# Two-layer attention and dense kernel: inverse roots of twelve norm chunks on DVE in place of ACT, and the first dense transposes ahead of an output projection

## The reference

```python
def _layernorm(x, axis=-1, eps=1e-05):
    m = jnp.mean(x, axis=axis, keepdims=True)
    v = jnp.var(x, axis=axis, keepdims=True)
    return (x - m) / jnp.sqrt(v + eps)
...
x = x + attn_a(_layernorm(x))   # 32 heads of 8, biases, softmax over all 1024 keys
x = x + ffn(_layernorm(x))      # silu(x @ w_gate) * (x @ w_up), 2 of each 4 kept by size, @ w_down
x = x + attn_b(_layernorm(x))   # 32 query heads, 8 key/value heads, a band of 128 keys masked
x = x + ffn(_layernorm(x))      # the same dense layer again
```

## Time and profile before

| | before |
|---|---|
| runs, median | 1659.77 us |
| the profiled execution, time | 1661.77 us |
| its span | 1659.80 us |
| PE busy | 1609.1 us, 97% |
| DVE busy | 1491.0 us, 90% |
| ACT busy | 1281.8 us, 77% |
| POOL busy | 266.8 us, 16% |
| mean granted PE clock | 0.991 |

### The profile page before, as it was taken

How to read it: one execution, slowest core, us unless ns; L and a number is a source line. 1 busy time by engine, 2 the same in 40 slices (tenths; PEclk the granted TensorE clock), 3 DMA queues, 4 the chain that set the end, 5 groups by cost and what they waited for, 6 DMA issues and landing times.

```text
span 1659.8 us, 39596 instructions
## 1 busy us (share of the span) xinstructions
PE 1609.1 (97%) x14128; PEld 636.9 (38%) x14128; DVE 1491.0 (90%) x2168; ACT 1281.8 (77%) x2424; POOL 266.8 (16%) x623
## 2 busy tenths in 40 slices
PE   6899999999999999999988999999999999999999
PEld 3322222222222223787653222222222222237877
DVE  6999999999999997787678999999999999937765
ACT  3399999999999998433224999999999999983321
POOL 1410000000000000000012222333332233320000
PEclk9989999999999999999998999999999999999999
DMA  6943344334354321200404232222222322112000
GB/s 160 296 98 70 63 76 84 63 64 84 69 139 87 73 60 44 64 1 0 117 15 132 59 66 57 51 51 65 57 55 62 62 57 51 55 49 58 14 13 26
DMA packets 72126, 114.70 MB, mean 69 GB/s; under 512 B 12464, under 2 KB 27824, under 8 KB 71984
## 3 DMA queue, kind: packets, MB, share of 16 engines
q1 hardware_dynamic: 71984, 112.63, 29.2%
HBM read 71.96 MB, written 40.63 MB: 68 GB/s over the span
## 4 chain that ended last, share of the span: by engine, by line
PE 54%; DVE 35%; issue 7%; ACT 1%; DMA 1%; SPq 0%; DVEq 0%; POOLq 0%; ACTq 0%
DVE mneg L1306 28%; PE psum L785 18%; PE psum L767 11%; PE psum L737 7%; PE psum L887 5%; PE psum L843 5%; PE psum L848 2%; PE psum L700 2%; PE psum L823 2%; PE psum L720 1%; PE psum L682 1%; DVE area L1356 1%; DVE area L1390 1%; DVE stats L1199 1%; DVE area L1340 1%
## 5 line engine op out<-in xcount | busy, mean ns | idle before, releaser
L1055 ACT ACTIVATE area<-psum 128x512 f32<-128x512 f32 x2048 | 1097.2, 600 | 42.1 <-PE psum L767 13.7
L785 PE MATMUL psum<-area 128*32 128x256 f32 x8192 | 655.2, 392 | 0.4 <-POOL area L1568 0.4
L767 PE MATMUL psum<-area 51*128 51x512 bf16 x2048 | 639.2, 385 | 2.5 <-DVE vsb_b L1256 1.4
L1312 DVE CUSTOM_DVE_ANT_0 xn<-psum,band 128x1024 f32<-128x1024 f32 x512 | 588.4, 1220 | 10.3 <-PE psum L737 9.3
L1306 DVE TENSOR_REDUCE mneg<-psum 128x1 f32<-128x1024 f32 x512 | 581.0, 1211 | 7.0 <-PE psum L737 6.9
L785 PEld LDWEIGHTS psum<-area 128*32 128x32 f32 x8192 | 162.1, 108 | 400.7 <-issue 259.1
L737 PE MATMUL psum<-area 48*128 48x512 bf16 x1024 | 301.6, 385 | 8.2 <-DVE mneg L1306 5.1
L767 PEld LDWEIGHTS psum<-area 51*128 51x128 bf16 x2048 | 141.0, 94 | 427.0 <-ACT area L1055 353.3
L737 PE MATMUL psum<-k_max_b,area 48*128 48x512 bf16 x1024 | 292.8, 385 | 5.4 <-DVE mneg L1312 4.7
L1549 POOL TENSOR_TENSOR mparts<-mneg,nought 128x16 bf16<-128x16 f32 x64 | 14.1, 221 | 742.3 <-DVE mneg L1306 501.1
L1100 ACT ACTIVATE area<-psum 128x512 f32<-128x512 f32 x64 | 38.2, 599 | 115.9 <-PE psum L848 115.8
(11 more groups left out here) (89 smaller groups left out, 1092.1 us busy)
## 6 DMA issues: line engine op xcount, KB each, us to landing
ctx_rows<-area SPq DMA_DIRECT2D x64, 256.0 KB, 2.1
area<-q_stacks SPq DMA_DIRECT2D x32, 384.0 KB, 6.8
area<-k_stacks SPq DMA_DIRECT2D x64, 192.0 KB, 5.6
area<-q_stacks_b SPq DMA_DIRECT2D x32, 384.0 KB, 5.3
area<-q_stacks SPq DMA_DIRECT2D x32, 192.0 KB, 4.6
area<-q_stacks_b SPq DMA_DIRECT2D x32, 192.0 KB, 3.4
area<-ctx_rows SPq DMA_DIRECT2D x16, 256.0 KB, 4.1
area<-inv_rows SPq DMA_DIRECT2D x16, 256.0 KB, 4.5
```

Source lines behind the costliest of these rows:

```text
L767: pe.matmul(psum[:, BANK_OF["exp", g, u, head], :], k_st[lo:lo + ROWS + PARTS, buf, 0 if a else head // 2, kt * P:(kt + 1) * P], q_st[lo:l ...
L785: mm = pe.matmul(psum[head * VW:(head + 1) * VW, BANK_OF["ctx", g, qh], cols], vaug[:, buf, kt, head, :], probs[:, u % PRING, head, cols], ...
L1055: act.activation(probs[:, u % PRING, head, :], psum[:, BANK_OF["exp", like, u, head], :], ACT.Exp, scale=SCALE).then_inc(bank_freed, 1)
L1312: dve.tensor_tensor_reduce(band_out[:, c % 2, :], slot, band[:, at:at + SEQ], 1.0, -3.0e38, ALU.add, ALU.max, mneg[:, qh, col:col + 1]).th ...
```

## The change

For k = 1, 2 and 3 ACT's square root and DVE's reciprocal are gone. In their place DVE's `invert_deviation` adds eps to the variance, makes a first guess of the inverse root from the bits of the number taken as an integer, and improves it by three Newton steps of three instructions each: eleven instructions on 128 x 4 elements, each of which waits for the one before (`root_step`). ACT's calls of `norm` for k = 1 to 3 go, k = 0 stays as it was. On PE `norm_transpose(2a + 1, 0)` now stands ahead of `project_out(a, 1)`, and on DVE `residue(2a + 1, 0)` ahead of `add_attention(a, 1)`. No DMA is added, removed or moved.

```diff
--- before.py
+++ after.py
@@ -20,6 +20,7 @@
 F32 = mybir.dt.float32
 BF16 = mybir.dt.bfloat16
 F32R = mybir.dt.float32r
+I32 = mybir.dt.int32
 ALU = mybir.AluOpType
 ACT = mybir.ActivationFunctionType
 AX = mybir.AxisListType
@@ -37,6 +38,8 @@
 SCALE = 1.0 / float(HD) ** 0.5
 EPS = 1e-5
 INNER = 1024
+FIRST_ROOT = 1597463007.0
+ROUNDS = 3
 BANK = 512
 HALF = SEQ // BANK
 
@@ -186,6 +189,8 @@
         mv = sb("mv", [P, BT, 2])
         std = sb("std", [P, BT])
         rstd = sb("rstd", [P, BT])
+        root_square = sb("root_square", [P, BT])
+        root_gain = sb("root_gain", [P, BT])
         eps = sb("eps", [P, 1])
         ident = sb("ident", [P, P])
         ident_bf = sb("ident_bf", [P, P], BF16)
@@ -318,7 +323,7 @@
         const_ready = sem("const_ready")
         const_step, ones_set, vaug_set = sem("const_step"), sem("ones_set"), sem("vaug_set")
         ln_stats, ln_mv, ln_sd, ln_rstd, ln_xn = (sem(s) for s in ("ln_stats", "ln_mv", "ln_sd", "ln_rstd", "ln_xn"))
-        ln_tr, ln_evac = sem("ln_tr"), sem("ln_evac")
+        ln_tr, ln_evac, root_step = sem("ln_tr"), sem("ln_evac"), sem("root_step")
         whole_hi, whole_split, xd_split = sem("whole_hi"), sem("whole_split"), sem("xd_split")
         proj_ready, hi_done, rest_done, mid_done, lo_done = (
             sem(s) for s in ("proj_ready", "hi_done", "rest_done", "mid_done", "lo_done"))
@@ -942,8 +947,8 @@
                 project_v(0, 0, v)
             for a in range(2):
                 attend(a)
+                norm_transpose(2 * a + 1, 0)
                 project_out(a, 1)
-                norm_transpose(2 * a + 1, 0)
                 if a == 0:
                     pe.wait_ge(wf_loaded, 48)
                 gate_up(a, 0, 0)
@@ -993,7 +998,7 @@
             def norm(k, c):
                 n, lo = 4 * k + c, c % 2 * CT
                 act.wait_ge(ln_mv, n + 1)
-                if n == 0:
+                if c == 0:
                     act.wait_ge(const_ready, 1)
                 act.activation(std[:, lo:lo + CT], mv[:, lo:lo + CT, 1], ACT.Sqrt, bias=eps[:]).then_inc(ln_sd, 1)
 
@@ -1121,7 +1126,6 @@
                     group(a, 2 * i + 1, 1)
                     group(a, 2 * i + 2, 2)
                 group(a, GROUPS - 1, GROUPS - 1, ahead=False)
-                norm(2 * a + 1, 0)
                 copy_ctx(a, GROUPS - 1, 1, GROUPS - 1)
 
             norm(0, 0)
@@ -1147,22 +1151,16 @@
             for a in range(2):
                 attend(a)
                 copy_transposed(2 * a + 1, 0)
-                norm(2 * a + 1, 1)
                 silu_and_size(a, 0, 0)
                 copy_transposed(2 * a + 1, 1)
                 silu_and_size(a, 0, 1)
                 silu_and_size(a, 1, 0)
-                norm(2 * a + 1, 2)
-                norm(2 * a + 1, 3)
                 silu_and_size(a, 1, 1)
                 copy_transposed(2 * a + 1, 2)
                 copy_transposed(2 * a + 1, 3)
-                if a == 0:
-                    norm(2, 0)
                 silu_and_size(a, 2, 0)
                 if a == 0:
                     copy_transposed(2, 0)
-                    norm(2, 1)
                     for i in range(3):
                         split_step(1, 0, i)
                 silu_and_size(a, 2, 1, turned=None if a else (2, 1))
@@ -1172,11 +1170,9 @@
                 silu_and_size(a, 3, 0)
                 silu_and_size(a, 3, 1)
                 if a == 0:
-                    norm(2, 2)
                     copy_transposed(2, 2)
                     for i in range(3):
                         split_step(1, 1, i)
-                    norm(2, 3)
                     copy_transposed(2, 3)
                     copy_turned(1, 0, 0, 0)
                     for i in range(3, PCH[1] + 1):
@@ -1203,12 +1199,36 @@
                     ins = dve.bn_aggr(mv[:, lo + t, :], stats[:, lo + t, :])
                 ins.then_inc(ln_mv, 1)
 
+            def invert_deviation(k, c):
+
+                n, cols = 4 * k + c, slice(c % 2 * CT, c % 2 * CT + CT)
+                s0 = (1 + 3 * ROUNDS) * (n - CH)
+                v, y, t, g = std[:, cols], rstd[:, cols], root_square[:, cols], root_gain[:, cols]
+                dve.wait_ge(ln_mv, n + 1)
+                dve.tensor_scalar(v, mv[:, cols, 1], EPS, None, ALU.add).then_inc(root_step, 1)
+                dve.wait_ge(root_step, s0 + 1)
+                dve.tensor_scalar(y.bitcast(I32), v.bitcast(I32), -0.5, FIRST_ROOT, ALU.mult, ALU.add
+                                  ).then_inc(root_step, 1)
+                for i in range(ROUNDS):
+                    dve.wait_ge(root_step, s0 + 3 * i + 2)
+                    dve.tensor_tensor(t, y, y, ALU.mult).then_inc(root_step, 1)
+                    dve.wait_ge(root_step, s0 + 3 * i + 3)
+                    dve.scalar_tensor_tensor(out=g, in0=t, scalar=-0.5, in1=v, op0=ALU.mult,
+                                             op1=ALU.mult).then_inc(root_step, 1)
+                    dve.wait_ge(root_step, s0 + 3 * i + 4)
+                    ins = dve.scalar_tensor_tensor(out=y, in0=g, scalar=1.5, in1=y, op0=ALU.add, op1=ALU.mult)
+                    ins.then_inc(ln_rstd if i == ROUNDS - 1 else root_step, 1)
+
             def scale(k, c):
                 n, lo = 4 * k + c, c % 2 * CT
-                dve.wait_ge(ln_sd, n + 1)
+                if k == 0:
+                    dve.wait_ge(ln_sd, n + 1)
                 if k == 2 and c == 2:
                     dve.wait_ge(stacks_stored[9], SD)
-                dve.reciprocal(rstd[:, lo:lo + CT], std[:, lo:lo + CT]).then_inc(ln_rstd, 1)
+                if k == 0:
+                    dve.reciprocal(rstd[:, lo:lo + CT], std[:, lo:lo + CT]).then_inc(ln_rstd, 1)
+                else:
+                    invert_deviation(k, c)
                 dve.wait_ge(ln_rstd, n + 1)
                 for t in range(CT):
                     if n >= 2 and t % 2 == 0:
@@ -1448,8 +1468,8 @@
                     dve.wait_ge(x_biased, 1)
                 add_attention(a, 0)
                 norm(2 * a + 1, 0)
+                residue(2 * a + 1, 0)
                 add_attention(a, 1)
-                residue(2 * a + 1, 0)
                 norm(2 * a + 1, 1)
                 invert_sums(a, 1)
                 hidden(a, 0, 0, follower=(0, 1))
```

## The result

| | runs shown | median | lowest to highest |
|---|---|---|---|
| kernel before, beside it | 6 | 1660.3 us | 1659.49 to 1665.77 |
| changed kernel | 6 | 1680.51 us | 1677.18 to 1683.82 |

The ratio is 1.0115, 95% interval [1.0103, 1.0127]: slower by some 20 us, where +10.6 was forecast. The direction was right, the size missed, and the range too. Three of the changed kernel's six times lie near 1677.4 and three near 1683.7; the profiled execution, 1683.82 with a span of 1681.8, is one of the longer ones.

What follows compares the result with a forecast made beforehand. It took PE (97% busy) and DVE's waits as the bound, not ACT's load; +8.30 us in the first dense layer and +2.33 in the second made +10.6 on 1659.77, so 1670.4 us, range 1665.8 to 1674.8.

Steps and rivals of the forecast that it cites:

- What bounds the kernel: Whole kernel: PE busy 97%, with 54% of the chain, DVE 35%, ACT 1%; ACT's load no bound, added DVE time can lose.
- (2,0): First dense layer, norm 2's first chunk: removed loads give DVE 0.59 us, scaling costs 1.89 more, so PE waits +1.30 us.
- (2,1): First dense layer, norm 2's second chunk: ACT's projection copy no longer stands behind the root, PE's idle goes, -0.68 us.
- The price of a Newton chain: On DVE, each norm chunk: eleven dependent instructions of 0.19 us, 2.12 us from last aggregation to scaling.
- 99 d - 8.2: Total change in us over nine chunks on the chain, d being the length of one Newton instruction; +13.1 at 0.215.
- (1,0), (3,0) and the order: Both dense layers' openings: chain fits DVE's idle time, gate matmuls start earlier, first gated product later: +0.82 and +0.87 us.
- (1,2) and (1,3): First dense layer, norm 1's last two chunks: both chains delay PE's row r2 at 736.48, +3.08 us.
- (2,2) and (2,3): First dense layer, norm 2's last two chunks: PE already idles behind DVE, each pays 1.89 in full, +3.78 us.
- (3,2) and (3,3): Second dense layer, norm 3's last two chunks: 3.08 us on DVE, less 1.62 of PE slack, +1.46 us.
- Rival 2: Newton chains on DVE: instructions are cheap, at 0.074 us spacing the sum is +0.2, 1660.0 us; chance 0.09.
- rival 3: Dense layers: ACT was what held them, so the change gains 8.5 us, to 1651.3; chance 0.04.
- rival 1: PE's waits at 736 and 758: clock falls in longer waits, 1 to 2 us each, two falls give 1673.3; chance 0.18.

## Why the prediction was wrong in size, point by point

- **What bounds the kernel**: right. Eleven loads went, 17.6 us of ACT's busy time in all, and DVE's waits set the end. What ACT's roots and loads gave back is in the terms of (2,0) and (2,1) below, and these came as forecast.
- **The price of a Newton chain**: right. 0.198 us an instruction for 0.19. The forecast's own formula, 99 d - 8.2, gives 11.4 at 0.198, and the ledger has 11.4; the single terms are off by 0.04 to 0.24.
- **(1,0), (3,0) and the order**: +0.91 and +0.94 for +0.82 and +0.87, and the first gate matmul at 671.09 without idle. One step of it was off: Silu's table load runs at 673.85 to 675.13, when the gate product is ready, not at 669. Nothing waited for it.
- **(1,2) and (1,3)**: +3.21 for +3.08. **(2,0)**: +1.36 for +1.30. **(2,1)**: -0.72 for -0.68, the wait at 777 gone. **(2,2) and (2,3)**: +1.96 and +2.03 for 1.89 each. **(3,2) and (3,3)**: +1.7 for +1.46.
- **Rival 2 and rival 3** fell: the spacing is 0.198 and nowhere near 0.074, and PE's long waits all name DVE.
- **The step that failed** is the clock. The sum took it as unchanged, and rival 1, whose mechanism is the one that happened, was given 0.18 and "two falls", 1 to 2 us each. A single place cost 0.85 to 2.67, near that price. The number of falls was wrong: four new stretches and three that grew, 10.6 us. The mechanism is not the whole of it either, since 3.0 of the 10.6 stand behind waits that the change left as long as they were, where the rival spoke of longer waits alone. I had asked only whether the waits at 736 and 758 would become long. But the waits before the first r2 of each layer, at 857 and at 880 grow too, and the earlier trace rows had shown what waits of 1.67 and 3.25 do, the second with its granted clock. "Both waits are a little shorter, with dense matmuls right before" was the argument against it, and it holds no weight: behind 3.34 and 2.95, straight after dense matmuls, the clock fell in both profiled executions of the changed kernel.
- The forecast did not count what the kernel before already loses to such falls, 8.6 us. That changes no term of the sum, but it would have shown how often a wait of 1.4 to 3.3 us has one behind it.

The Trainium skill, "TensorE: Matmul & The Clock Gate", section "What's actually happening", says that for modeling the penalty of the clock's ramp is under 1% of a typical kernel's span. The trace of the kernel before agrees, with 8.6 us or 0.5%; that of the changed kernel does not, with 22.2 us or 1.3%, and there the measurement decides.

**What stays open.** Why one execution of the changed kernel takes 1676 and another 1687 us isn't explained: the profiled two differ by 7.5 us, 5 of them clock. Nor is it known why the clock falls behind a wait in one kernel or execution and not in another, for waits of the same length. The fillers were never tried one place at a time, so what each place gives back is only the ledger's reading. That the 5 us stalls are instruction fetch rests on q14's packets and on the padding; where the code must lie wasn't tried, and no trace shows an instruction being waited for.

## What to carry to other kernels

Before DVE work is put on a chain that PE waits for, list the waits of PE it lengthens, and price each twice: once what it gets longer, and once a possible 0.9 to 2.7 us lost to matmuls at the 1.2 GHz level behind it; here the two parts were nearly equal, 11.4 and 10.6. The second price is not certain at any one place: it came behind some waits that had not changed, and stayed away behind one of 2.87 us. A root by Newton steps (2.21 us in eleven dependent instructions) paid here where the engine that works it out was idle: at two such places, together with the new order, it won 1.5 us, at all twelve chunks it lost 17 to 20. A few matmuls that nothing reads, shorter than the wait they stand in, held the clock and won back 8 to 11 us; longer than the wait, they lost it all again.

## What was not expected of the hardware

- Waits of the same length (3.34 and 3.35 at row r2) were followed by low clock for 4 us in one execution and for 8 in the other, and that at 1521 by a fall in one and none in the other. A wait of 2.5 us that all kernels have near 800 had full clock behind it in the kernel before and a fall in the changed one.
- 36 instructions fewer on DVE, 24 of them ahead of attention b, brought three stalls of 5 us in a loop that the edit doesn't touch. 36 idle writes ahead of it took them away again, and made attention b 20 us shorter (1694.65 to 1674.66 us).
- A float32 matmul of 128 columns by the identity takes two records and some 0.23 us (5.07 us for 22), where one of a transpose's eight takes 0.14 (1.09 for 8).
